# An attention and mixture-of-experts block: 38 dense units laid into the slots of the last batch's heads, ScalarE squaring and GpSimd multiplying by the gates

## The reference

```python
# r, k, v: (B, T, C); decay per batch and channel; f is both k and v
ek, ekv = exp(min(f, 30)), exp(min(f, 30)) * f
nf, df = forward scans of a = a * decay + (ekv, ek);  nb, db = the same backwards
num = nf + nb - ekv + exp(min(u + f, 30)) * f
den = df + db - ek + exp(min(u + f, 30))
mixed = sigmoid(r) * num / max(den, 1e-8) * (0.8 + 0.2 * tf)

x = x + attention(mixed(x))          # qkv, softmax(4 * q k^T), values, output projection
y = mixed2(x)                        # second block, other w and u
score = sigmoid(y @ gate_w.T)        # 64 experts in 8 groups; top 4 groups, top 6 experts
w = normalised scores of the six, times 2.5, else 0
routed = sum over e of w[t, e] * relu(y @ w1[e].T)**2 @ w2[e].T
shared = relu(y @ shared_up.T)**2 @ shared_down.T
out = x + routed + shared
```

## Time and profile before

| what | value |
|---|---|
| median of three runs | 408.05 us |
| the profiled execution | 405.65 us |
| its span | 403.8 us |
| TensorE matmuls, busy | 317.7 us (79%) |
| VectorE busy | 322.9 us (80%) |
| ScalarE busy | 201.2 us (50%) |
| GpSimd busy | 129.5 us (32%) |
| first head's maximum | 42.48 us |
| first maximum of the last batch | 159.54 us |
| first up of unit 0 | 192.89 us |
| mean granted TensorE clock | 0.897 |

### The profile page before, as it was taken

How to read it: one execution, slowest core, us unless ns; L and a number is a source line. 1 busy time by engine, 2 the same in 40 slices (tenths; PEclk the granted TensorE clock), 3 DMA queues, 4 the chain that set the end, 5 groups by cost and what they waited for, 6 DMA issues and landing times.

```text
span 403.8 us, 6023 instructions
## 1 busy us (share of the span) xinstructions
PE 317.7 (79%) x1552; PEld 244.3 (61%) x1552; DVE 322.9 (80%) x623; ACT 201.2 (50%) x373; POOL 129.5 (32%) x117
## 2 busy tenths in 40 slices
PE   0071369677954897768988897999999999999994
PEld 0050247455733585545666675888888788888882
DVE  6979997986699477886568995888888888888883
ACT  4112125434552256466455553666666666656651
POOL 3428443306061002011322342434334334334331
PEclk9995559758985798997999998999999999999999
DMA  6959707803380068300543444566556666656531
GB/s 199 164 71 119 166 2 93 111 11 52 55 106 2 13 94 105 108 10 24 173 144 117 157 168 145 163 188 192 194 181 194 177 200 188 199 182 191 195 139 52
DMA packets 36150, 50.89 MB, mean 126 GB/s; under 512 B 5218, under 2 KB 17954, under 8 KB 36130
## 3 DMA queue, kind: packets, MB, share of 16 engines
q1 hardware_dynamic: 36130, 50.65, 51.4%
HBM read 39.16 MB, written 1.33 MB: 100 GB/s over the span
## 4 chain that ended last, share of the span: by engine, by line
PE 54%; DVE 29%; issue 7%; ACT 5%; POOL 2%; DMA 1%; DVEq 0%; ACTq 0%; SPq 0%; POOLq 0%
DVE scan L731 7%; PE ps L1258 7%; PE ps L1260 7%; PE ps L1269 6%; PE ps L1271 6%; PE ps L1259 6%; PE ps L1270 6%; DVE mx L796 5%; PE ps L1129 4%; PE ps L1172 3%; PE ps L1140 2%; DVE q_st L949 2%; DVE scan L1053 2%; PE ps L1159 2%; DVE den L744 2%
## 5 line engine op out<-in xcount | busy, mean ns | idle before, releaser
L446 POOL TENSOR_TENSOR scan<-scan 128x512 f32<-128x512 f32 x68 | 73.2, 1076 | 137.9 <-ACT scan L574 136.2
L1058 DVE TENSOR_TENSOR qk_lo<-scan,qk_hi 128x512 fp32r<-128x512 f32 x68 | 69.3, 1019 | 31.3 <-ACT qk_hi L581 31.3
L574 ACT ACTIVATE scan<-ps 128x512 f32<-128x512 f32 x68 | 40.7, 598 | 49.8 <-PE ps L1260 49.6
L1140 PE MATMUL ps<-k_st,q_st 96*128 96x256 f32 x128 | 35.6, 395 | 30.8 <-DVE mx L796 20.3
L1269 PE MATMUL ps<-qk_hi,k_st 128*128 128x512 f32 x136 | 54.7, 402 | 4.5 <-DVE qk_lo L1058 4.3
L1258 PE MATMUL ps<-hid_hi,k_st 128*128 128x512 f32 x136 | 54.4, 400 | 2.0 <-DVE q_st L949 2.0
L567 ACT ACTIVATE k_st<-clip 128x512 fp32r<-128x512 f32 x68 | 42.8, 631 | 25.3 <-PE ps L1271 25.3
L1260 PE MATMUL ps<-hid_hi,q_st 128*128 128x512 f32 x136 | 54.0, 397 | 0.0
L1271 PE MATMUL ps<-qk_hi,q_st 128*128 128x512 f32 x136 | 53.7, 395 | 0.0
L1270 PE MATMUL ps<-qk_lo,k_st 128*128 128x512 f32 x136 | 53.6, 394 | 0.0
L1259 PE MATMUL ps<-hid_lo,k_st 128*128 128x512 f32 x136 | 53.6, 394 | 0.0
(11 more groups left out here) (117 smaller groups left out, 451.4 us busy)
## 6 DMA issues: line engine op xcount, KB each, us to landing
clip<-in_tiles SPq DMA_DIRECT2D x68, 256.0 KB, 3.1
ex<-gates SPq DMA_DIRECT2D x136, 128.0 KB, 2.9
q_st<-qk_hi SPq DMA_DIRECT2D x16, 128.0 KB, 3.9
q_st<-qk_lo SPq DMA_DIRECT2D x16, 128.0 KB, 4.5
k_st<-qk_hi SPq DMA_DIRECT2D x16, 128.0 KB, 5.3
k_st<-qk_lo SPq DMA_DIRECT2D x16, 128.0 KB, 6.2
f_sb<-in_fT SPq DMA_DIRECT2D x4, 256.0 KB, 8.8
x_sb<-in_xT SPq DMA_DIRECT2D x4, 256.0 KB, 9.6
```

The lines of the kernel that those rows point to most:

```text
L446: g.tensor_tensor(sq[:, k], relu[:, k], relu[:, k], ALU.mult).then_inc(sq_ready, 1)
L1058: TT(act_lo[:, k], act[:, k], act_hi[:, k].bitcast(F32), ALU.subtract).then_inc(act_lo_ready, 1)
L1140: last = mm(bank_s(n)[:, qt], q_st[0:MAXROW, slot(b, h // HB), h % HB, qt * P:(qt + 1) * P], k_st[0:MAXROW, slot(b, h // HB), h % HB, :], ...
```

## The change

Everything before the last batch runs in 48 slots, one for each head of batches 0 to 2: slot g has the maximum of head g, the scores of head g+2, and the shifted scores of a head ten slots back (`LAG`). The projections, tails and recurrences stand at fixed slots. The last batch and the first 38 units (`HEAD`) share 43 slots s = 0 to 42: heads' maxima in 0 to 15, shifted scores up to 25, units from slot 4 on (units 0 and 1 in slots 4 and 5, none in 6, unit s-5 from slot 7). For that, scores and shifted scores have one bank each from the last batch on, and units below 12 one bank for h. The tail of batch 2 is in slots 11 to 16, that of batch 3 in 27 to 32. The router runs twice, on four tiles each: in slots 0 to 3, and in 33 to 36. The gates are stored twice. The other 30 units stay a loop.

In every unit ScalarE now does the square behind the relu, GpSimd the product with the gates, and VectorE no longer has that product. The rest of q and k of batches 1 to 3 comes from two matmuls with minus the identity and a ScalarE pass, the bias of v from a one-row matmul, and ScalarE moves v. The spread gates come with one DMA a unit instead of two. Tiles that only need space share it with others.

```diff
-HEAD = 18
+RT = 2 * QT
+LAG = 10
+ENTRY = 4
+GAP = 1
+ALONE = 12
...
+HEAD = NT + RING
...
         def bank_s(n):
-            return ps[:, n % 2, :].rearrange("p (t k) -> p t k", t=QT)
+            return ps[:, n % 2 if n < H * (B - 1) else 0, :].rearrange("p (t k) -> p t k", t=QT)
 
         def bank_t(n):
-            return ps[:, 2 + n % 2, :].rearrange("p (t q) -> p t q", t=QT)
+            return ps[:, 2 + n % 2 if n < H * (B - 1) - HB else 2, :].rearrange("p (t q) -> p t q", t=QT)
 
...
-            return ps[:, 2 + 2 * oc + half, :]
+            return ps[:, ((3, 5), (2, 4))[half][oc], :]
+
+        def unit_bank(n):
+            return n % 2 if n >= ALONE else 1
+
+        def unit_at(s):
+            n = s - ENTRY if s < ENTRY + SHARED else s - ENTRY - GAP
+            return n if n >= 0 and (s < ENTRY + SHARED or n >= SHARED) else None
+
+        def head_slot(n):
+            early = H + HB <= n < 2 * H
+            return H + HB + LAG + (n - H - HB) // 2 if early else n + LAG
+
+        def shifted_at(g):
+            return [n for n in range(H * B) if head_slot(n) == g]
+
+        def values_at(g):
+            return [n // 4 for n in range(3, H * B, 4) if head_slot(n) + 1 == g]
+
+        def tail_slot(b):
+            return head_slot(H * b + H - 1) + 2
...
-            def square(n, k):
-
-                pool.wait_ge(relu_ready, n + 1)
-                g.tensor_tensor(sq[:, k], relu[:, k], relu[:, k], ALU.mult).then_inc(sq_ready, 1)
...
+            def gated(n, k, s, turns):
+
+                pool.wait_ge(sq_ready, n + 1)
+                pool.wait_ge(ld_spread[s], 16 * turns)
+                if not isinstance(n, int) or n >= 2:
+                    pool.wait_ge(act_hi_ready, n - 1)
+                    pool.wait_ge(act_lo_ready, n - 1)
+                g.tensor_tensor(act[:, k], sq[:, k], spread[:, s], ALU.mult).then_inc(act_ready, 1)
+
+            for s in range(HEAD + ENTRY + GAP):
+                n = unit_at(s)
+                if n is not None:
+                    gated(n, n % 2, n % RING, n // RING + 1)
+                if s == tail_slot(2) - H * (B - 1) + 3:
...
+                    gated(n, k % 2, (HEAD + k) % RING, i + (HEAD + k) // RING + 1)
...
 
                 sc.wait_ge(h_ready, n + 1)
+                if isinstance(n, int) and n == 0:
+                    sc.wait_ge(numden_ready, 4 * B)
+                bank = unit_bank(n) if isinstance(n, int) else k
+                a.activation(relu[:, k], bank_h(bank), ACT.Relu).then_inc(relu_ready, 1)
                 if not isinstance(n, int) or n >= 2:
-                    sc.wait_ge(sq_ready, n - 1)
-                a.activation(relu[:, k], bank_h(k), ACT.Relu).then_inc(relu_ready, 1)
+                    sc.wait_ge(act_ready, n - 1)
+                sc.wait_ge(relu_ready, n + 1)
+                a.activation(sq[:, k], relu[:, k], ACT.Square).then_inc(sq_ready, 1)
 
...
+            for g in range(H * (B - 1)):
+                b, s = g // H, g % H
+                for n in shifted_at(g):
+                    probabilities(n // H, n % H, n % H + 1)
+                if s == 2:
...
+            for s in range(HEAD + ENTRY + GAP):
+                n = unit_at(s)
+                for m in shifted_at(H * (B - 1) + s):
+                    probabilities(m // H, m % H, m % H + 1)
...
+                    evacuate_w(1)
+                if n is not None:
+                    rectify(n, n % 2)
+                    if n > 0:
+                        round_act(n - 1, (n - 1) % 2)
+                    split_hi(n + 2, (n + 2) % RING, (n + 2) // RING + 1)
...
+            for g in range(H * (B - 1)):
+                b, s = g // H, g % H
+                maximum(b, s)
...
-            def gated(n, k, s, turns):
-
-                dve.wait_ge(sq_ready, n + 1)
-                dve.wait_ge(ld_spread[s], 32 * turns)
-                if not isinstance(n, int) or n >= 2:
-                    dve.wait_ge(act_hi_ready, n - 1)
-                    dve.wait_ge(act_lo_ready, n - 1)
...
-            for n in range(HEAD):
-                if n > 0:
-                    low_act(n - 1, (n - 1) % 2)
-                gated(n, n % 2, n % RING, n // RING + 1)
-                split_lo(n + 2, (n + 2) % RING)
...
+            for s in range(HEAD + ENTRY + GAP):
+                n = unit_at(s)
+                if s < H:
+                    maximum(3, s)
+                if s == 0:
+                    low_max(2, 1)
...
+                if s < 4:
+                    for _ in range(6):
+                        next(route_now, None)
...
+                    if n > 0:
+                        low_act(n - 1, (n - 1) % 2)
+                    split_lo(n + 2, (n + 2) % RING)
...
+            def subtract_high(b, w):
+
+                job = ("qk"[w], b)
+                pe.wait_ge(qk_hi_ready, 4 * b + 2 * w + 2)
+                for t in range(KC):
+                    last = mm(job_bank(job)[:, t * S:(t + 1) * S], minus[:], qk_hi[:, w, t], start=False, stop=True,
+                              skip_group_check=True)
+                last.then_inc(rest_ready, 1)
...
                 if h % HB == 0:
                     pe.wait_ge(ld_rows[slot(b, h // HB)], 32 * turn(b, h // HB))
                 if n >= 2:
...
-                if not isinstance(n, int) or n >= 2:
+                bank = unit_bank(n) if isinstance(n, int) else k
+                if not isinstance(n, int) or n > ALONE + 1:
                     pe.wait_ge(relu_ready, n - 1)
+                elif n == 0:
+                    pe.wait_ge(max_ready, H * (B - 1))
+                elif n == ALONE:
+                    pe.wait_ge(max_ready, H * B)
+                else:
+                    pe.wait_ge(relu_ready, min(n, ALONE))
...
+            for g in range(H * (B - 1)):
+                b, s = g // H, g % H
+                for n in shifted_at(g):
+                    shifted_scores(n // H, n % H)
+                if g + 2 <= H * (B - 1):
+                    scores((g + 2) // H, (g + 2) % H)
+                for m in values_at(g):
+                    values(m // 4, m % 4)
...
+            for s in range(HEAD + ENTRY + GAP):
+                n = unit_at(s)
+                for m in shifted_at(H * (B - 1) + s):
+                    shifted_scores(m // H, m % H)
+                if s + 1 < H:
+                    scores(B - 1, s + 1)
```

More of the change, by code:

```diff
@@ L361, in _ @@
[L361 to L370 removed]
+            for n in range(RING, RING + SHARED):
+                next_spread(n, 0, n, n % RING)
@@ new lines, in _ @@
+            for s in range(HB - 1, HEAD + 1):
+                if s + 1 >= 2 * RING and s + 1 < HEAD:
+                    n = s + 1
+                    next_raw(n, n % NT, n % RING)
+                n = s - 1
+                if n == NT + SHARED:
+                    store_gates(1)
+                if n >= RING + SHARED:
+                    next_spread(n, n // NT, n % NT, n % RING)
+                if s == HB - 1:
+                    load_rows(B - 1, 0)
+                if s == H - 1:
+                    load_rows(B - 1, 1)
@@ L443, in square @@
-            def square(n, k):
-                pool.wait_ge(relu_ready, n + 1)
-                g.tensor_tensor(sq[:, k], relu[:, k], relu[:, k], ALU.mult).then_inc(sq_ready, 1)
-            square(0, 0)
-            square(1, 1)
-            with pool.Fori(1, NT) as i:
-                for k in range(2):
-                    pool.wait_ge(act_ready, 2 * i + k - 1)
-                    square(2 * i + k, k)
+            for b in range(2):
+                sums(b + 1, 1, 1)
+                sums(b + 1, 1, 0)
+                products(b + 2)
+                sums(b + 2, 0, 1)
+                sums(b + 2, 0, 0)
+                add_logs1(b + 2)
@@ L455, in _ @@
+            for n in range(UNITS - 2, UNITS):
+                gated(n, n % 2, n % RING, n // RING + 1)
         @block.scalar
@@ L465, in _, with exponentials @@
             a.activation(tex[:], tsum[:], ACT.Exp, scale=-1.0).then_inc(setup_exp, 1)
-            def exponentials(b):
-                if b > 0:
+            def exponentials(b, first, last):
+                if b > 0 and first == 0:
                     sc.wait_ge(esum_ready, 4 * b)
@@ new lines, in _ @@
+                if b < 2 and s == 15:
+                    reciprocal1(b + 2)
+                for c in range(2):
+                    t = g - tail_slot(c)
+                    if t == 2:
+                        evacuate_o_ch(c)
+                    if t == 5:
+                        second_exp(c)
+                    if t == 6:
+                        second_rec(c)
+                    if t == 7:
+                        round_hidden(c)
+                    if t == 8 and c == 1:
+                        gate_exp(c)
@@ L1092, in loop @@
+            assert next(route_now, None) is None
+            result(0)
             def loop(first, units):
@@ L1355, in _ @@
+            for n in range(UNITS - 2, UNITS):
+                up(n, 1, n % 2, n % RING)
```

(1 more changed line is left out.)

786 lines of the change are left out of this document (366 added, 420 removed).

## The result

The changed kernel takes **632.53 us** (median of four runs, 627.64 to 637.12) against 406.88: a ratio of 1.550, interval 1.538 to 1.562. The forecast was 442 us, in a range of 414 to 460. The direction was right, the size was not: the change cost about 226 us, and the forecast held 34. No rival came near.

A forecast was written before the change was run, and what follows sets the result against it. TensorE was taken to bound the old unit loop at 2.76 us; in the new one `low_act`, held behind GpSimd, makes 3.08. Stage terms summed to a span of 439.7 us, plus 1.85 gave 442; range 414 to 460.

The forecast's parts named there:

- The gates' DMA: Spread gates, one 256 KB DMA a unit: hidden by a ring of four units; up to 3 us uncovered for unit 2.
- B: The 48 slots of batches 0 to 2: 97 us, the middle of 88 to 106, instead of 117.06 before.
- E: Clock cost in slots 4 to 15: 5 us, a third of the way between bounds 0 and 17.
- F to H: From slot 15 through the last 30 units: 35.1, 66.3 and 92.4 us, at 3.08 us a loop unit.
- A: Start of the kernel to the first maximum: 42.5 us, as the list ahead of it changes little.
- C: Slots 0 to 3: 18.1 us, of which the router of four tiles 12.6 and the gates' turn through TensorE 1.0.
- D: Slot 4's maximum to slot 15's: 71.7 us, nine of its 11 intervals at 6.46 us.
- the chain of 6.46 us: Common slots: one maximum to the next through scores, up, relu, square, GpSimd's product, `low_act`, `split_lo`; 6.46 us a slot.
- rival 3: Half clock through slots 4 to 15 and the 48 earlier slots at their upper end: 454 to 463 us; chance 0.14.
- The hold: In units, VectorE's `low_act` ends 0.55 us after the GpSimd product it meets, about 1.3 us instead of 0.68.
- rival 1: Units and slots: VectorE isn't held behind GpSimd, the loop stays 2.76 us a unit, total 418 us; chance 0.17.
- Rival 2: Slots and units run at TensorE's own pace, slots about 5.0 us or less, total 389 us; chance 0.10.

## Why the prediction was wrong, step by step

- **The gates' DMA** (costed at nothing, or at up to 3 us for one unit) is the step that failed, and it is 145 us. I took 2.9 us from the earlier trace rows for a DMA of 128 KB to 64 partitions from one row and gave it to a DMA from two rows. I counted bytes and issues, and did not ask on how many engines the new form runs. All three runs agree: with the form of before 487, with one row 484, and in the kernel before, given the new form, 614. It is not the only step that failed: the 45 us over the forecast that are left come from B, E and F to H below.
- **A**: 41.3; right. **C**: 18.0 against 18.1, by luck. In slots 0 to 3 of the run with two DMAs the router took some 9.9 us of VectorE (170.97 to 183.26, less three maxima and one `split_lo`) and not 12.6, and VectorE waited 4.2 us (3.4 for ScalarE's step of the row of maxima, 0.8 for its rounding of weights) where I had put 1.0. (With the single DMA these slots took 23.)
- **B**, 97 taken of 88 to 106: measured 124.0 in the run with two DMAs, outside the bounds, and the largest of the three terms that are over. One thing was misread before the sum was made: the last batch's first maximum stands at 155.27 in the trace of before, and 159.54 is its third, so that this stage took 112.8 us and not 117.06. The changed stage is 11 us longer than that, though VectorE is busy for 77.9 us only. The bounds came from busy times, which a chain through several engines does not heed. With two buffers for q and k it was 119.6 in one profiled execution and 115.0 in another, 3.3 us of that by the clock of one stretch. The loads of the stacks aren't the cause of what is left, since half of them left it at 115.1. That it is TensorE's pieces at half clock (granted 0.64 to 0.80 here), between which heads wait in order, is shown only for those 3.3 us; for the rest it is argued from the chain, and the cause of the stage's length stays open.
- **D**: the chain of 6.46 us was right link by link, and the cut of one link gave 26 us back in these slots.
- **E**, 5 taken of 0 to 17: D and E together are 10.6 over, so it should have been near 16. In most slots of this stretch (0.73 granted) up ran at half clock, 0.43 us a matmul, the upper end's case and rival 3's. I had weighed it by the two windows of the earlier trace rows that lay nearest.
- **F to H**: 3.24 to 3.29 us a unit instead of 3.08. The sum had both units of a pair alike; in the kernel before with the new engines the products start in turn 2.55 and 3.83 us apart, with 2.77 between. The hold (1285 ns for the product, 1212 to 1390 for `low_act`) is as forecast, so rival 1 is out; so is the smaller product of 1.07 us.
- **Rival 2** never had its condition: in the run with two DMAs slots with a unit took 7.4 to 10.3 us. With the link cut most took 4 to 6, and the whole was still 17 us over the kernel before.

## What to carry to other kernels

Before two DMAs are merged into one, look at what dimension now stands outermost on both sides, and cost the new form as unknown unless a row has that form. The DMA that kept to two of 16 engines here also delayed the next one in its queue, from 3.1 to 14.5 us. When a stage is laid over another, follow each engine's list round the loop: what matters is not the sum of the work but whether a step that waits stands ahead of one that doesn't need to. Before a difference of a few us between two profiled executions is given to an edit, look whether it lies where the edit is. And where two engines hold each other up, the order in a third one's list can choose which step is held.

## What the runs showed of the hardware that was not expected

- A DMA of 256 KB with two rows as its source's outermost dimension: 48 GB/s at 0.13 to 0.14 of 16 engines, for some 5 us; the same bytes from one row landed after 3.4 us.
- Behind it the issue of the next DMA takes 4.7 to 4.8 us on SyncE, instead of 0.33 in the run with one row, while the share of busy engines stays at two of 16.
- The same matmuls, in two kernels that are equal up to there, took 10.1 us at a granted clock of 0.50 and 6.8 at 0.93.
- Merging the two DMAs of 128 KB in the harmless form (one row) gained at most 3 us: 484.4 against 487.2, within the spread of these runs.
